# Retention of a decoder layer as a loop on every engine, three batches a turn, with its inputs copied to three fixed tiles by GpSimd

## The reference, cut to what matters

```python
qk = x @ Wqk + bqk;  v = x @ Wv + bv;  n = x @ Wn + bn      # x: (16, 256, 128), 16 heads of 8
q, k = split(qk.reshape(b, s, 2, 16, 8))
scores = einsum('bthd,bshd->bhts', q, k)
attn = scores * tril(ones(s, s)) / exp(n)[..., None]        # no softmax: linear attention
ctx = einsum('bhts,bshd->bthd', attn, v)
return ctx @ Wo + bo
```

## Time and profile before

| | |
|---|---|
| median of 3 runs | 1857.0 us |
| profiled execution | 1858.44 us, its span 1856.6 us |
| mean granted TensorE clock | 0.978 |
| retention, first matmul to the barrier behind it | 26.4 to 168.8 us |
| cross attention with its layer norm | 168.8 to some 1065 us |
| feed-forward, two layers | to the end |

### The profile page before, as it was taken

The page is one execution under the profiler, slowest core; times in us unless marked ns, Lnnn a source line. Parts: engine busy times, 40 slices in busy tenths (PEclk is TensorE's granted clock), DMA queues, the critical chain, the costliest instruction groups (busy, mean ns, idle before and its releaser), DMA issues. The chain is left out here.

```text
span 1856.6 us, 67818 instructions
## 1 busy us (share of the span) xinstructions
PE 1705.8 (92%) x27988; PEld 1021.8 (55%) x27988; DVE 1028.4 (55%) x3242; ACT 1465.9 (79%) x2635; POOL 445.3 (24%) x353
## 2 busy tenths in 40 slices
PE   7897799999999999999999968989989889889888
PEld 5674455555555555555555425656653356556633
DVE  5454633333433333343331069999964499899854
ACT  4332699999998999999999858999973389899932
POOL 1003100000000000000000047767710377677400
PEclk9898999999999999999999989999999999999999
DMA  1000311111111111111110030111110011111100
GB/s 60 3 3 26 105 48 62 50 46 59 62 62 46 51 49 60 45 62 62 55 36 17 23 95 20 35 31 25 29 27 11 0 27 25 35 24 32 32 15 34
DMA packets 47468, 73.87 MB, mean 40 GB/s; under 512 B 8400, under 2 KB 38224, under 8 KB 47184
## 3 DMA queue, kind: packets, MB, share of 16 engines
q1 hardware_dynamic: 47184, 69.85, 12.1%
HBM read 21.08 MB, written 2.10 MB: 12 GB/s over the span
## 5 line engine op out<-in xcount | busy, mean ns | idle before, releaser
L651 ACT ACTIVATE x_probs<-x_pss 128x1024 f32<-128x1024 f32 x832 | 807.4, 1023 | 47.2 <-PE x_pss L572 31.3
L586 PE MATMUL x_acc<-x_probs,x_v 128*32 128x256 f32 x6656 | 437.6, 380 | 0.4 <-issue 0.4
L572 PE MATMUL x_pss<-x_qx,x_kx 32*128 32x256 bf16 x9984 | 348.2, 270 | 11.0 <-ACT x_probs L651 7.5
L572 PEld LDWEIGHTS x_pss<-x_qx,x_kx 32*128 32x128 bf16 x9984 | 221.6, 93 | 196.7 <-ACT x_probs L651 183.6
L586 PEld LDWEIGHTS x_acc<-x_probs,x_v 128*32 128x32 f32 x6656 | 206.2, 110 | 93.5 <-issue 9.3
L1253 ACT ACTIVATE l_prob<-l_sim,l_neg_top,l_inv_norm 128x128 f32<-128x128 f32 x512 | 247.1, 490 | 5.4 <-DVE l_neg_top L1147 4.4
L698 DVE COPY x_vnext<-x_psp 128x128 f32<-128x128 f32 (+1 forms) x199 | 59.3, 298 | 315.3 <-PE x_psp L550 312.2
L879 POOL TENSOR_TENSOR l_turned_half<-l_raw,l_tabB 128x512 f32<-128x512 f32 x128 | 180.7, 1433 | 65.2 <-ACT l_raw L1212 64.8
L627 POOL COPY x_zq<-zT 128x256 f32 (+1 forms) x15 | 6.0, 402 | 757.6 <-PE x_psp L557 691.9
L889 POOL TENSOR_TENSOR l_direct<-l_direct,l_turned_half 128x1024 f32<-128x1024 f32 x64 | 156.6, 2446 | 0.0
L1139 DVE CUSTOM_DVE_ANT_0 l_sim<-l_pss,w_window 128x128 f32<-128x128 f32 x512 | 118.0, 285 | 3.3 <-issue 1.9
(11 more groups left out here) (183 smaller groups left out, 2631.9 us busy)
## 6 DMA issues: line engine op xcount, KB each, us to landing
x_kx<-x_kp SPq DMA_DIRECT2D x96, 208.0 KB, 2.4
x_cT<-in_context SPq DMA_DIRECT2D x16, 832.0 KB, 4.4
x_qx<-x_qp SPq DMA_DIRECT2D x48, 192.0 KB, 2.3
l_vmid<-l_vt SPq DMA_DIRECT2D x64, 128.0 KB, 2.3
xT<-in_x SPq DMA_DIRECT2D x8, 256.0 KB, 4.9
shifted<-zT SPq DMA_DIRECT2D x32, 64.0 KB, 2.0
hs<-zT SPq DMA_DIRECT2D x32, 64.0 KB, 2.0
out_x<-xT SPq DMA_DIRECT2D x8, 256.0 KB, 2.0
```

The costliest lines, as they stand in the source:

```text
L572: ins = pe.matmul(pss[bank(k, 2 * p + r // 2)][:, r % 2, e, :], kx[par][rows, g, j * P:(j + 1) * P], qx[par][rows, g, a * S:(a + 1) * S], ...
L586: ins = pe.matmul(acc[32 * r:32 * r + 32, 0:S], v[:, j, g, r, :], probs[SLOT[p]][r // 2][:, r % 2, e, :], start=(u == 0), stop=(u == UNITS ...
L651: act.activation(probs[SLOT[p]][y][:, :, :, :], pss[bank(k, 2 * p + y)][:, :, :, :], ACT.Sigmoid, scale=HD ** -0.5).then_inc(weighed, 1)
```

## The change

The four engines' programs in `retention` get a common frame `turns`: batches 0 to 2 are written out, batches 3 to 11 are a loop of three turns of three batches, batches 12 to 15 are written out. In the loop the batch number is a register's value and the buffer number u is a constant. `past` and `left` decide at build time whether a wait or a step is needed, so that the body of the loop holds them all.

[...] So GpSimd copies batch n of zT (128x256) to `staged[n % 3]`: three copies before its first batch, then one a batch, three batches ahead. `project` waits for the copy (z_staged) and reads `staged` in place of zT. GpSimd waits with the copy until the projection that read the same buffer is done. It also gets an instruction of one column (pool_beat) ahead of its four copies of v, with a wait for the one of the batch before (beaten). ScalarE's `take_out` still writes to zT, at a computed address. In `mix` the wait for masks and v moves ahead of the last of the three state matmuls.

```diff
+        staged = [sb(f"staged{u}", [P, S]) for u in range(NB)]
+        z_staged, beaten, pool_beat = sem("z_staged"), sem("beaten"), sb("pool_beat", [P, 1])
+        def turns(eng, body):
+            for n in range(3):
+                body(n, n % NB)
+            with eng.Fori(0, 3) as i:
+                for u in range(NB):
+                    body(3 * i + 3 + u, u)
+            for n in range(12, B):
+                body(n, n % NB)
...
-            def project(n):
-                u, at = n % NB, slice(n * S, (n + 1) * S)
-                if n >= 1:
+            def project(n, u):
+                pe.wait_ge(z_staged, n + 1)
+                if past(n, 1):
                     pe.wait_ge(k_ready, n)
...
-                pe.matmul(psk, w["wk"][:, :], zT[:, at], start=True, stop=True).then_inc(k_projected, 1)
+                pe.matmul(psk, w["wk"][:, :], staged[u][:, :], start=True, stop=True).then_inc(k_projected, 1)
...
                 for c, first in ((2, True), (1, True), (3, False)):
                     t, e = divmod(c, 2)
+                    if c == 3:
+                        pe.wait_ge(v_set, HL * (n + 1))
+                        pe.wait_ge(masked, HG * (n + 1))
                     pe.matmul(pso[e][:, t * CK:(t + 1) * CK], state[:, c - 1, :], q32[u][:, c * CK:(c + 1) * CK],
                               start=first, stop=False, skip_group_check=True)
-                pe.wait_ge(v_set, HL * (n + 1))
-                pe.wait_ge(masked, HG * (n + 1))
...
+            def stage(n, u):
+                if past(n, NB):
+                    pool.wait_ge(kv_projected, n - NB + 1)
+                pool.tensor_copy(staged[u][:, :], zT[:, ds(n * S, S)]).then_inc(z_staged, 1)
+            def turn(n, u):
                 pool.wait_ge(kv_ready, n + 1)
-                if n >= NB:
+                if past(n, NB):
                     pool.wait_ge(mixed, n - NB + 1)
+                if past(n, 1):
+                    pool.wait_ge(beaten, n)
+                pool.tensor_tensor(pool_beat[:, :], w["bq"][:, :], w["bk"][:, :], ALU.add).then_inc(beaten, 1)
...
+                if left(n + 3):
+                    stage(n + 3, u)
+            for n in range(3):
+                stage(n, n)
+            turns(pool, turn)
```

More of the change, by code:

```diff
@@ L257, in project @@
                     pe.wait_ge(q_ready, n)
-                pe.matmul(psnq[:, 0, :], w["wn"][:, :], zT[:, at], start=True, stop=True)
-                pe.matmul(psnq[:, 1, :], w["wq"][:, :], zT[:, at], start=True, stop=True).then_inc(nq_projected, 1)
-                if n >= 1:
+                pe.matmul(psnq[:, 0, :], w["wn"][:, :], staged[u][:, :], start=True, stop=True)
+                pe.matmul(psnq[:, 1, :], w["wq"][:, :], staged[u][:, :], start=True, stop=True).then_inc(nq_projected, 1)
@@ L277, in score, with sum_states @@
                 ins.then_inc(scored, 1)
[L279 to L281 removed]
+            def sum_states(n, u):
+                x = kv[u]
                 pe.wait_ge(kv_ready, n + 1)
[L283 removed]
+                if past(n, 1):
                     pe.wait_ge(o_ready, 2 * n)
@@ L309, in mix, with keys, inverse, split_queries @@
                 ins.then_inc(mixed, 1)
[L311 to L318, removed]
+            def turn(n, u):
+                score(n, u)
+                sum_states(n, u)
+                if left(n + 2):
+                    project(n + 2, (u + 2) % NB)
+                mix(n, u)
+            project(0, 0)
+            project(1, 1)
+            turns(pe, turn)
         @block.scalar
         def _(act):
-            def keys(n):
+            def keys(n, u):
                 act.wait_ge(k_projected, n + 1)
-                act.activation(k32[n % NB][:, :], psk, ACT.Identity, bias=w["bk"][:, 0:1]).then_inc(k_ready, 1)
-            def inverse(n):
+                act.activation(k32[u][:, :], psk, ACT.Identity, bias=w["bk"][:, 0:1]).then_inc(k_ready, 1)
+            def inverse(n, u):
                 act.wait_ge(nq_projected, n + 1)
-                act.activation(inv_n[n % NB][:, :], psnq[:, 0, :], ACT.Exp, bias=nbn[:, 0:1], scale=-1.0).then_inc(n_exp, 1)
-            def split_queries(n):
+                act.activation(inv_n[u][:, :], psnq[:, 0, :], ACT.Exp, bias=nbn[:, 0:1], scale=-1.0).then_inc(n_exp, 1)
+            def split_queries(n, u):
                 act.wait_ge(q_ready, n + 1)
                 for m in range(HL):
-                    act.activation(qm[n % NB][:, m, :], q32[n % NB][:, :], ACT.Copy,
+                    act.activation(qm[u][:, m, :], q32[u][:, :], ACT.Copy,
                                    scale=w["rowmask"][:, m:m + 1]).then_inc(qm_ready, 1)
@@ L344, in _, with turn, tokens, queries @@
             act.wait_ge(neg_bn, 1)
-            for n in range(2):
[L346 to L355, removed]
+            def turn(n, u):
+                if left(n + 2):
+                    keys(n + 2, (u + 2) % NB)
+                    inverse(n + 2, (u + 2) % NB)
+                take_out(n)
+                if left(n + 2):
+                    split_queries(n + 2, (u + 2) % NB)
+            for n in range(2):
+                keys(n, n)
+                inverse(n, n)
+                split_queries(n, n)
+            turns(act, turn)
         @block.vector
         def _(dve):
-            def tokens(n):
+            def tokens(n, u):
                 dve.wait_ge(kv_projected, n + 1)
-                dve.tensor_tensor(kv[n % NB][:, :, :], pskv[:, :, :],
+                dve.tensor_tensor(kv[u][:, :, :], pskv[:, :, :],
                                   w["bkv"][:, :].unsqueeze(1).broadcast_to([P, 2, 2 * D]), ALU.add).then_inc(kv_ready, 1)
-            def queries(n):
+            def queries(n, u):
                 dve.wait_ge(n_exp, n + 1)
-                dve.scalar_tensor_tensor(q32[n % NB][:, :], psnq[:, 1, :], w["bq"][:, 0:1], inv_n[n % NB][:, :],
+                dve.scalar_tensor_tensor(q32[u][:, :], psnq[:, 1, :], w["bq"][:, 0:1], inv_n[u][:, :],
                                          ALU.add, ALU.mult).then_inc(q_ready, 1)
@@ L379, in keep_states, with turn @@
                                   ALU.mult).then_inc(state_ready, 1)
-            for n in range(2):
-                queries(n)
-                tokens(n)
-            for n in range(B):
+            def turn(n, u):
                 mask(n, 0)
```

36 lines of the change are left out of this document (21 added, 15 removed).

## The result

The changed kernel takes 1844.2 us (median of 5 runs, 1841.1 to 1848.9) against 1860.7 us before in the same session: ratio 0.991, interval 0.9885 to 0.994. The forecast was 1850.4 us with a range down to 1845.5, so it came out faster than the range. The profiled pair (1848.9 after, 1858.4 before) is 9.5 us apart. The profiled execution of the changed kernel is the slowest of its five, so what happens in a stage is read from the traces, and how much the kernel gained from the medians.

The account below looks back on a forecast made before the run. The retention was taken as bound by PE, losing time to late instruction fetches (idle) and a lower clock. -9.6 + 0.4 + 0.9 + 0.5 + 1.2 = -6.6 us from 1857.0 gave 1850.4 us, range 1845.5 to 1857.5.

Parts of the forecast that it names:

- rival A: Retention loop: the body is not kept and each turn fetches anew, +9.3 us, hence 1866.3 us or more; chance 0.05.
- 23 packets became 15: Sign on q8 in the retention: 23 packets minus 8 or 9, none from the loop's second turn on.
- 9.6 less loop ends: Batches 6 to 11 run from the kept body, 49.85 to 40.26 us, gain 9.6; loop ends on PE cost 0.9.
- the branch takes 220 and 246 ns: Sign at the retention's loop ends: PE's COMPARE_BRANCH takes under 0.3 us.
- PE waits for a staged input only once: Sign in the retention: no wait of PE on z_staged but the first, with GpSimd's copies two batches ahead.
- registers (0.5): Register instructions in the retention's loop on PE: 0.05 us a batch over 9 batches, +0.5 us, upper bound 3.5.
- the moved wait (1.2): The wait moved in mix delays the last weight loads: +1.2 us, bounds 0 and 3.5.
- rival B: Stalls go, but small costs reach their upper bounds: -0.9 us, hence 1856.1; chance 0.22 together with an in-between 1853.
- the straight batches gain nothing: Batches 0 to 5 and 12 to 15 of the retention were summed with no gain.
- No gain, and a new position of the packets' borders: Batches 12 to 15, straight code again: gain 0, with instruction packets' borders falling elsewhere.
- rival C: Moved packet borders also help batches 12 to 15 and later code: 4 us more, -10.6, hence 1846.4; chance 0.27.
- the start: PE's first projection in the retention waits for a GpSimd copy of 402 ns: +0.4 us, bounds 0.4 and 0.8.

Follow-up runs that it names:

- experiment 1: The kernel before with 80 small memsets on VectorE in the first layer norm: 1850.2 us, ratio 0.994 to the kernel before.
- 3: The kernel after with all 16 batches written out, no loop, staging and moved wait kept: 1863.0 us, ratio 1.0004 to the kernel before.
- 128 on TensorE: The kernel before with 32 one-column matmuls (128 TensorE instructions) at the start of the first norm: 1863.7 us, ratio 1.0014.
- 5: The kernel after run once more, unchanged: 1845.3 us, ratio 0.994 to the kernel before.
- 20: The kernel after with 20 small memsets on VectorE in the first layer norm: 1848.4 us, ratio 0.994 to the kernel before.
- 25: The kernel after with 25 small memsets on VectorE in the first norm: 1870.1 us in one run, 1869.0 for the kernel before beside it.
- 30: The kernel after with 30 small memsets on VectorE in the first layer norm: 1855.5 us, ratio 0.997 to the kernel before.
- 45: The kernel after with 45 small memsets on VectorE in the first layer norm: 1868.6 us, ratio 1.0035 to the kernel before.
- ScalarE: The kernel after with 50 small activations on ScalarE, 25 in each of the first two layer norms: 1842.4 us, ratio 0.991.
- TensorE: The kernel after with 12 one-column matmuls (48 TensorE instructions) in the second norm: 1841.0 us, ratio 0.989 to the kernel before.
- experiment 6: Two fills of one-column matmuls: 12 in the kernel after's second norm, 1841.0 us; 32 in the kernel before's first norm, 1863.7 us.

## Why the prediction was wrong

**Right.** The mechanism of the retention: the body of 1,100 TensorE instructions is kept (rival A is out), 23 packets became 15, batches 6 to 11 fell by 9.1 us in the profiled pair (9.6 less loop ends was forecast), the branch takes 220 and 246 ns, PE waits for a staged input only once. The small costs were small: an inner batch in the loop takes 6.72 us against 6.71, and the two that cross a loop end 7.06 and 6.82, and PE's wait for masks is 2.1 us in two pieces, as before (2.0); so the terms for registers (0.5) and the moved wait (1.2) are nearly nothing, and rival B's upper bounds were far too high. Over more executions the picture gets clearer. From the first score of batch 0 to that of batch 15 the retention takes, in the mean,

| | profiles | batches 3-5 | 6-11 | 12-14 | whole |
|---|---|---|---|---|---|
| straight code (before, 1, 3, 128 on TensorE) | 4 | 28.0 | 49.1 | 25.3 | 126.5 us |
| three turns (after, 5, and the fills 20, 25, 30, 45, ScalarE, TensorE) | 8 | 28.9 | 40.8 | 24.3 | 118.1 us |

That is 8.4 us less, nearly all of it in batches 6 to 11. That the straight batches gain nothing was the sum's assumption, and it holds in the mean.

**Wrong.** The step that failed is the one on what lies outside the loop: "No gain, and a new position of the packets' borders". I asked what moved borders do to TensorE, and only in the retention's last batches and by chance (rival C). The same shortening moved VectorE's code by 34 instructions, in a part of the program that the diff doesn't touch, and there it decides whether a loop's body is kept. That term was missing from the sum: 11.5 us in the profiled pair, 10.6 us by putting it into the kernel before (experiment 1), 9.9 us by taking it out of the kernel after (30 memsets, 0.53%; 4.3 us against the kernel after as it ran again). I had even read that loop, but only its first layer, where a turn took 67.6 to 68.6 us, and concluded from it that the loop is kept. The second layer runs the same code at another place, at 74.24 and 70.76 us, and would have shown that the conclusion is not about the body's size alone.

A second missing term goes the other way. The cross attention's head came to lie 25 instructions ahead of a border of TensorE's packets: 323.25 to 324.95 us, and 322.75 with the head moved. In the mean, seven profiles with that position give 325.0 us and four of straight code 322.7: +2.3 us.

A third term was there and too small: the start, forecast at 0.4 us with an upper bound of 0.8. The wait itself is of that size. PE stands for 2.08 us ahead of its first matmul in place of 1.64. But in all 11 profiles with the staging the granted clock is then at its lower level (0.50, 1.2 GHz) for about 3 us or more, and from ScalarE's first instruction to the first score it takes 6.5 to 7.2 us. In the three profiles that project straight from zT it takes 6.2 us in the kernel before, also partly at the lower clock, and 4.6 us twice at full clock (experiment 1, and 128 on TensorE in 6). In the mean of the eight profiles of three turns and of these three, that is +1.6 us. That the longer wait brings the lower clock is suggested by 11 of 11 against 1 of 3, and no run isolates it.

With all three, the sum comes near: -8.4 in the retention, +1.6, +2.3, and -9.9 to -11.5 in the second layer are -14.4 to -16.0; measured were 16.5 us less, and 13.6 when the kernel after ran again. It is not closer than that, since stages that the diff leaves alone differ between profiles too: from the last batch's score to the cross attention's loop it takes 104.2 to 109.1 us.

What I had set out to forecast, the change without its side effect, is the comparison of two kernels in the same state of that loop. With 30 memsets (loop fetched anew, as before) against the kernel before it is 0.9966, -6.3 us (-10.0 to -2.6). The kernel after against the kernel before with 80 memsets (both kept) is 1844.2 against 1850.2 us, -6, with the first session of the kernel after, and nothing with its second (ratios 0.9943 and 0.9943). The stages give -8.4 + 1.6 + 2.3 = -4.5. So the forecast of -6.6 lies within the interval of the first comparison, at the edge of what the three say together. That it comes so close is partly luck: it left out +2.3 and some +1.2 of the start, and charged 1.7 for registers and the moved wait that were not paid. Rival C's 1846.4 is near the result for a reason that is not its own: in the profiled execution batches 12 to 14 got 5.0 us longer, not shorter.

The staging gives TensorE operands at fixed addresses in the loop. Not all of them need that. In the feed-forward loop TensorE reads its moving operand at an address computed from the loop's register, in the kernel before as in the kernel after:

```python
ins = pe.matmul(to[:, :], w["w1"][:, m * P:(m + 1) * P], hs[:, ds(n * CH, CH)], ...)
```

```profile
L1414 PE MATMUL g_mean<-hs,w_w x64: 592/592/667, 1398.0 to 1831.8; 128*128 x48, 128*128 128x512 f32 x16
L1414 PEldq FUSED_REGOPS  x12: 55/55/60, 1404.9 to 1818.1; - x12
```

The last row has the address: one register instruction of 55 ns in each of the 12 passes. By this, three of the five matmuls of `project`, those where zT is the moving operand, could read zT without a copy; for the two where it is the stationary operand no run shows it. A loop without the staging, or with the first batches alone projected from zT, was not tried.

The Trainium skill, in "Runtime: NRT & Kernel Launch", Instruction fetch mechanics, gives most engines 512 instructions of their own memory, and TensorE 2048, refilled in blocks of 256. Four blocks of 128 would be 512, and a body of 322 that is kept on three blocks and not on four agrees with that if one is taken by what is fetched next; no run here shows that last step. The packets of 8 KB disagree with the page's blocks of 256 for these engines, and those of TensorE (0.38 MB in 23) agree.

**Open.** Why VectorE's refetch costs between 3.1 and 10.3 us a turn, when VectorE stands for 2.7 to 3.5 us behind the branch in all six profiles with such a loop, was not separated. A lower clock afterwards may be part of it (0.95 to 0.98 in the turns of some 73 us and more, 1.00 in those of 70.6 and 70.8), and so may the engines that wait for VectorE. Why ScalarE's packets cost next to nothing was not tried either. And the true start of the bodies is known only to within 3 instructions.

## What to carry to other kernels

A change in the length of one engine's code is a change to every later loop on that engine: before summing, list each loop's body on each engine, every copy of it apart, and look at the instruction queues in those stretches. A shorter code can win or lose some ten us elsewhere, so a small gain or loss of an edit should be checked by moving the code with idle instructions before it is credited to the edit. A small wait added ahead of TensorE's first matmul should be looked up with the granted clock behind it, and not be counted by its length alone. Where straight code is limited by fetching, as TensorE's short matmuls are here, let the loop cover as many batches as it can (four turns in place of three, 118.1 to 111.5 us).

## What the runs showed that I had not expected

- VectorE keeps a loop body of 322 instructions or fetches it at every loop end, by its position alone: 20 idle instructions ahead leave it, 25 throw it out, 45 throw out both layers' (1844 to 1869 us for the same work).
- ScalarE does the same with 291 instructions, and five of the six turns in which its packets come alone take 67.5 us, as without them; the sixth takes 68.6.
- A back branch to a place close ahead of a packet's border pays two fetches in a row (2.99 and 2.80 us of idle in the kernel after); both stalls stand in all seven profiles with this position.
- Two executions of the same retention code differ by up to 9 us there (124.1 and 114.9 us, the second with the fill of experiment 6 behind it; 7.5 us for one whole program run twice), by which packets come late and the half clock behind them. One profiled pair would have told that the loop gained 1.4 us.
- The copy of 0.4 us ahead of the first projection goes with about 3 us or more at the lower clock in every profile that has it; without it, two of three profiles stay at full clock there.
